# Self and cross attention as one loop over 32 head pairs, with the work between the two loops placed beside pairs of another batch

## Chip, cores and metric

The kernel runs on one core of a Trainium2 chip. The time is device microseconds of that core for one execution; lower is better. Engines: PE (TensorE), DVE (VectorE), ACT (ScalarE), POOL (GpSimd) and SP (SyncE, which issues the DMA here). Each engine works through its own list of instructions in order, and waits for the others at semaphores.

## What is computed

Two blocks on x (2 batches, 512 rows, 128 features) and a context (2 x 154 x 96), all float32. The first block is a small cross attention with 16 heads of 8 with layernorm, GELU feed-forward and residual; the change leaves it as it is. The second block is:

```python
x = _attn(_ln(x, g1, b1), _ln(x, g1, b1), Wq1, Wk1, Wv1, Wo1, bo1) + x   # self: 512 keys
x = _attn(_ln(x, g2, b2), context, Wq2, Wk2, Wv2, Wo2, bo2) + x          # cross: 154 keys
x = _geglu_ff(_ln(x, g3, b3), Wp, bp, Wf, bf) + x                        # a * gelu(gate) @ Wf
```

with 16 heads of 64 in `_attn`, softmax over the keys, and an output projection (1024 to 128). Batches never meet: what batch 1 does in self attention is independent of what batch 0 does in cross attention.

## The kernel before

The 16 heads are taken as 8 pairs, so an attention has 16 pairs (two batches of 8). Each attention is one loop over its pairs. Scores are computed transposed (keys on partitions) in `ph.units` chunks, 4 for self attention (128 keys each) and 2 for cross (77 each). The steps of a pair, with the lines that the profile shows:

- PE `project` (L1011, L1012): queries and keys of a pair, two pairs ahead, into a bank of the ring ST
- ACT `leading` (L487, or L489 and L490 in cross) rounds them into R; DVE `trailing` (L703, or L705 and L706) writes the rest and frees that bank
- PE `scores_max` (L1023) computes the scores of the next pair once for their maxima, DVE `maxima` (L715, L717) reduces them, PE `turn_pair` (L1032) transposes the maxima, ACT `maxima_rows` (L496) copies them
- PE `scores` (L1043) and `less_maxima` (L1052), ACT `exponentials` (L503) into PT, POOL sums them (L384, L388)
- PE `weigh` (L1063) multiplies with the values into PV, half a pair behind; ACT `weighted` (L510) copies PV into AT
- PE `denominators` (L1077) every second pair; after a batch's eight pairs DVE `inverse` (L725) takes the reciprocals, ACT and DVE split them (L515, L729), PE `spread_inverse` (L1086) spreads them over the features, DVE `normalise` (L736) multiplies AT

The ring ST has two PSUM tensors. Every user of it is in one fixed order, and each use waits until the use before the last one is freed. A second ring of two, M, serves the maxima.

For batch 0 the inverse is done inside the loop (pairs 9 to 11), for batch 1 behind it. Between the two loops stand, in this order: inverse and normalisation of batch 1, the values of the context (L1005), the output projection of both batches (`project_out`, L972), and for each batch the residual (L669, L768) and layernorm (`layernorm`, L645 to L659, with ACT's logarithm and exponential L466 and L467 in its middle), the transposes of the result XC (`turn`, L982) and ACT's scaling (L473). Only then does cross attention begin. Behind the cross loop the same steps are followed by GEGLU: `wp` products (L1142, L1143), ACT's Gelu (L558), DVE's product (L783), the last projection (L972) and the output.

Of the kernel before, what the change touches and what calls it, by code (L numbers as in the profile page):

```python
# [22 lines left out]
PAIRS = H // 2  # L23

# [13 lines left out]
def build(nc, a, out):  # L38
    ctx = ExitStack()
    with ctx:  # L40
# [100 lines left out]
        class Phase:  # L141

            def __init__(self, name, rows_of_chunk, chunks):
# [12 lines left out]
                self.den = sem(f"{name}_den")  # L156
                self.rec = sem(f"{name}_rec")
                self.rhi = sem(f"{name}_rhi")
                self.rlo = sem(f"{name}_rlo")
                self.bc = sem(f"{name}_bc")  # L160
                self.norm = sem(f"{name}_norm")

            def spread(self, c):

                return range(4 * c // self.units, 4 * (c + 1) // self.units)

        self_att = Phase("self", P, 4)
        cross_att = Phase("cross", SC, 2)
        self_att.first_turn, cross_att.first_turn = 0, NPAIR


# [4 lines left out]
        o_read = [sem(f"o_read{i}") for i in range(3)]  # L176
# [20 lines left out]
        units, freed = [], {}  # L197

        def unit(key, semaphore, count):
            freed[key] = (semaphore, count)  # L200
            units.append(key)

        for n in range(3):
            unit(("q0", n), full_done, n + 1)
        for n in range(4 * TB):
            unit(("m0", n), m0_free, n + 1)
        for n in range(B * 4):
            for u in range(4):
                unit(("s0", n, u), exp0_done, 4 * n + u + 1)

        def pair_units(ph):
            order = [("proj", 0), ("proj", 1), ("turn", 0)]
            for i in range(NPAIR):
                for c in range(0, ph.units, 2):
                    order += [("st", i, c), ("st", i, c + 1)]
                    if c + 2 == ph.units and i + 2 < NPAIR:
                        order.append(("proj", i + 2))
                    if i == 11:
                        order += [("bc", 0, m) for k in (c, c + 1) for m in ph.spread(k)]
                if i + 1 < NPAIR:  # L220
                    order.append(("turn", i + 1))
            order += [("bc", 1, m) for m in range(4)]
            for key in order:
                if key[0] == "proj":
                    unit((ph.name,) + key, ph.lo, key[1] + 1)
                elif key[0] == "turn":
                    unit((ph.name,) + key, mrow_set, ph.first_turn + key[1] + 1)
                elif key[0] == "bc":
                    unit((ph.name,) + key, ph.norm, 4 * key[1] + key[2] + 1)
                else:  # L230
                    unit((ph.name,) + key, ph.exp, key[1] * ph.units + key[2] + 1)

        unit(("o", 0), o_read[0], B)
        unit(("t", 0), xn_done[0], B)
        for n in range(B * 2):
            unit(("w1", n), gelu_done, 2 * (n + 1))
        unit(("w2",), w2_read, B)
        unit(("t", 1), xn_done[1], B)
        for t in range(NT):
            unit(("v", 0, t), (va_done if t % 2 == 0 else vd_done)[0], t // 2 + 1)  # L240
        pair_units(self_att)
        for t in range(4):
            unit(("v", 1, t), (va_done if t % 2 == 0 else vd_done)[1], t // 2 + 1)
        unit(("o", 1), o_read[1], B)
        unit(("t", 2), xn_done[2], B)
        pair_units(cross_att)
        unit(("o", 2), o_read[2], B)
        unit(("t", 3), xn_done[3], B)
        for n in range(B * 4):
            unit(("wp", n), glu_done, n + 1)  # L250
        unit(("wf",), y_done, B)
        place = {key: n for n, key in enumerate(units)}


        turn0_bank, max_bank = [0], []
        uses = 5
        for n in range(2 * 4 * TB):
            max_bank.append(uses % 2)
            uses += 1
        turn0_bank.append(uses % 2)  # L260
        uses += 1
        for ph in (self_att, cross_att):
            for n in range(2 * ph.units * NPAIR):
                max_bank.append(uses % 2)
                uses += 1

        def bank(key):
            return ST[place[key] % 2]
# [28 lines left out]

        @block.sync
        def _(sp):
# [23 lines left out]

            sp.wait_ge(self_att.proj, NPAIR)
            load("wv2", Wv[0:C, :], a["wv2"])
# [11 lines left out]
        def _(pool):  # L337
# [36 lines left out]
            def sums(ph):  # L374

                for i in range(NPAIR):
                    p = PT1[0:ph.KC, i % 2]
                    s = psums[0:ph.KC, i % 4]
                    pool.wait_ge(ph.exp, ph.units * i + 2)
                    if i >= 4:  # L380
                        pool.wait_ge(ph.den, i // 2 - 1)
                    elif ph is self_att:
                        pool.wait_ge(den0_done, 4 * B)
                    ins = pool.tensor_tensor(s, p[:, 0], p[:, 1], ALU.add)  # L384
                    for c in range(2, ph.NC):
                        link(ins)
                        pool.wait_ge(ph.exp, ph.units * i + c + 1)
                        ins = pool.tensor_tensor(s, s, p[:, c], ALU.add)  # L388
                    ins.then_inc(ph.sum, 1)

            sums(self_att)
            sums(cross_att)

        @block.scalar
        def _(act):
# [66 lines left out]
            def gain_bias(n, g, c):  # L462

                for b in range(B):
                    act.wait_ge(var_done[n], b + 1)
                    link(act.activation(lnv[:, :, :], mv[:, :, 1:2], ACT.Ln))  # L466
                    act.activation(rstd[:, :, :], lnv[:, :, :], ACT.Exp, scale=-0.5).then_inc(rs_done[n], 1)  # L467
                    scale_features(n, g, c, b)

            def scale_features(n, g, c, b):  # L470

                act.wait_ge(t_done[n], b + 1)
                act.activation(xnT[:, b * N:(b + 1) * N], bank(("t", n))[:, b, :], ACT.Identity,  # L473
                               scale=cols[:, g:g + 1], bias=cols[:, c:c + 1]).then_inc(xn_done[n], 1)

            def values(n, tiles, r):
                for t in range(0, tiles, 2):
                    act.wait_ge(v_done[n], t + 1)
                    act.activation(V[0:r, t, :].rearrange("p (u n) -> p u n", u=2), bank(("v", n, t))[0:r],
# [728 lines left out]
```

## Time and profile before

| what | value |
|---|---|
| median of 3 runs | 610.33 us (609.9 to 610.92) |
| the profiled execution, its own time | 609.28 us |
| its span, first to last instruction | 607.4 us |
| PE busy | 534.2 us (88%) |
| DVE, ACT, POOL busy | 276.2, 239.9, 186.2 us |
| mean granted clock of PE | 0.86 of 2.4 GHz |

The span is what the trace covers; all durations below are read against it. Self attention's loop runs from about 175 to 381 us, cross attention's from about 422 to 546 us.

### The profile page before, as it was taken

What the parts mean: (1) busy time and instruction counts of PE and PEld (TensorE: products, weight loads), DVE (VectorE), ACT (ScalarE), POOL (GpSimd) and SP (SyncE); (2) the same over time, 40 slices, a digit from 0 to 9 for tenths busy, and PEclk for the clock granted to TensorE, in tenths of its full rate; (3) what the DMA queues carried; (4) which work ended last, traced back from release to release, by engine and by line L of the source; (5) the groups of instructions that cost most, each with busy time, mean ns of one, the idle gap of its engine ahead of it and who ended that gap; (6) DMA issues with size and microseconds to landing.
All of it is one profiled execution on the core that took longest, in us unless ns stands there. A gap on an engine that the chain in (4) does not pass through costs nothing.

```text
span 607.4 us, 7004 instructions
## 1 busy us (share of the span) xinstructions
PE 534.2 (88%) x2824; PEld 273.4 (45%) x2824; DVE 276.2 (45%) x541; ACT 239.9 (39%) x321; POOL 186.2 (31%) x105
## 2 busy tenths in 40 slices
PE   6889979948778999999999999595799999986797
PEld 3563311226335445455444543274455454435745
DVE  1663430163445555455656550524434355515533
ACT  4433334224223555445544454011355555440131
POOL 4024333200002646656664467000133433330000
PEclk9955555559796999999999999598799999996979
DMA  9300000000000000000000020001000000000001
GB/s 279 127 0 2 0 1 1 1 0 0 0 1 1 2 1 0 1 1 1 0 1 1 2 87 1 0 1 35 0 1 1 2 0 2 1 1 0 1 0 36
DMA packets 7839, 8.95 MB, mean 15 GB/s; under 512 B 544, under 2 KB 6112, under 8 KB 7808
## 3 DMA queue, kind: packets, MB, share of 16 engines
q1 hardware_dynamic: 7808, 8.51, 4.5%
q8 instruction: 23, 0.38, 0.3%
q14 instruction: 8, 0.07, 0.0%
HBM read 7.98 MB, written 0.52 MB: 14 GB/s over the span
## 4 chain that ended last, share of the span: by engine, by line
PE 82%; DVE 13%; ACT 2%; issue 1%; POOL 1%; DMA 1%; SPq 0%; DVEq 0%; POOLq 0%
PE PV L1063 14%; PE ST L1043 11%; PE ST L972 7%; PE ST L1011 6%; PE M L1023 5%; PE PV L933 5%; PE ST L1005 4%; PE ST L1052 4%; PE ST L1032 3%; PE ST L1012 3%; PE DEN L944 3%; PE DEN L1077 3%; PE ST L916 2%; DVE AT L736 2%; PE M L861 2%; PE ST L1142 1%
## 5 line engine op out<-in xcount | busy, mean ns | idle before, releaser
L384 POOL TENSOR_TENSOR psums<-PT 128x1024 f32<-128x1024 f32 (+1 forms) x32 | 75.8, 2370 | 261.5 <-ACT PT L503 261.5
L503 ACT ACTIVATE PT<-ST 128x1024 f32<-128x1024 f32 (+1 forms) x96 | 93.8, 1022 | 44.4 <-PE ST L1052 44.3
L715 DVE TENSOR_REDUCE maxw<-M 128x1 f32<-128x512 f32 x128 | 82.4, 686 | 50.7 <-PE M L1023 50.5
L1063 PE MATMUL PV<-PT,V 128*64 128x512 f32 (+1 forms) x384 | 92.8, 604 | 0.8 <-ACT AT L510 0.8
L1043 PE MATMUL ST<-R 64*128 64x512 f32 (+1 forms) x576 | 86.7, 403 | 1.2 <-DVE R L706 0.6
L388 POOL TENSOR_TENSOR psums<-psums,PT 128x1024 f32<-128x1024 f32 x32 | 75.6, 2362 | 20.8 <-ACT PT L503 19.5
L1043 PEld LDWEIGHTS ST<-R 64*128 64x128 f32 (+1 forms) x576 | 51.4, 176 | 15.8 <-issue 1.6
L1023 PE MATMUL M<-R 64*128 64x512 f32 (+1 forms) x256 | 47.3, 377 | 6.2 <-DVE maxw L715 3.7
L459 ACT ACTIVATE PT<-ST 77x1024 f32<-77x1024 f32 x32 | 31.8, 1018 | 47.8 <-PE ST L916 47.8
L372 POOL TENSOR_TENSOR psums<-PT 77x1024 f32<-77x1024 f32 x12 | 28.1, 2351 | 68.2 <-ACT PT L459 40.8
L1063 PEld LDWEIGHTS PV<-PT,V 128*64 128x64 f32 (+1 forms) x384 | 23.5, 136 | 48.8 <-issue 42.3
L717 DVE TENSOR_REDUCE maxw<-M 128x2 f32<-128x308 f32 x64 | 27.5, 473 | 37.9 <-PE M L1023 37.8
L496 ACT ACTIVATE mrows<-ST 128x512 fp32r<-128x512 f32 x32 | 19.2, 599 | 54.2 <-PE ST L1032 54.2
L1011 PE MATMUL ST<-xnT,Wq 128*128 128x512 f32 x64 | 38.0, 677 | 2.5 <-DVE V L694 1.5
L1052 PE MATMUL ST<-mrows,onesr 64*128 64x512 f32 (+1 forms) x192 | 39.8, 399 | 0.0
L1023 PEld LDWEIGHTS M<-R 64*128 64x128 f32 x256 | 26.0, 192 | 30.4 <-DVE maxw L715 18.1
L933 PE MATMUL PV<-PT,V 77*32 77x512 f32 x128 | 30.7, 1061 | 3.7 <-DVE AT L613 3.7
L510 ACT ACTIVATE AT<-PV 128x512 f32<-128x512 f32 x32 | 19.1, 598 | 36.1 <-PE PV L1063 36.1
L703 DVE TENSOR_TENSOR R<-ST,R 128x1024 fp32r<-128x1024 f32 x16 | 19.6, 1225 | 28.5 <-ACT R L487 28.5
L972 PEld LDWEIGHTS ST<-Wo,AT 128*128 128x128 f32 x256 | 30.8, 202 | 1.6 <-issue 1.3
L972 PE MATMUL ST<-Wo,AT 128*128 128x128 f32 x256 | 30.9, 286 | 0.4 <-DVE AT L736 0.4
L982 PE MATMUL ST<-ident,XC 128*128 128x128 f32 x32 | 7.4, 374 | 23.3 <-DVE XC L659 23.3
(138 smaller groups left out, 625.1 us busy)
## 6 DMA issues: line engine op xcount, KB each, us to landing
Wq<-in_wq SPq DMA_DIRECT2D x2, 512.0 KB, 7.0
Wo<-in_wo SPq DMA_DIRECT2D x2, 512.0 KB, 6.5
xnT<-in_xT SPq DMA_DIRECT2D x2, 256.0 KB, 3.6
psums<-in_sel SPq DMA_DIRECT2D x1, 512.0 KB, 6.9
X<-in_x SPq DMA_DIRECT2D x1, 512.0 KB, 8.2
w<-in_w SPq DMA_DIRECT2D x2, 256.0 KB, 8.3
Wv<-in_wv SPq DMA_DIRECT2D x1, 512.0 KB, 8.9
Wk<-in_wk SPq DMA_DIRECT2D x1, 512.0 KB, 7.7
```

The costliest lines, as they stand in the source:

```text
L384: ins = pool.tensor_tensor(s, p[:, 0], p[:, 1], ALU.add)
L388: ins = pool.tensor_tensor(s, s, p[:, c], ALU.add)
L459: act.activation(PT0[0:SC, n % 2, u % 2, 2 * (u // 2):2 * (u // 2) + 2, :], bank(("s0", n, u))[0:SC, :, :], ACT.Exp, scale=HD0 ** -0.5).th ...
L503: act.activation(PT1[0:ph.KC, i % 2, c], bank((ph.name, "st", i, c))[0:ph.KC, :, :], ACT.Exp, scale=HD ** -0.5).then_inc(ph.exp, 1)
L715: ins = dve.tensor_reduce(maxw[:, i % 2, c, HD * h:HD * h + 1], m[:, :], AX, ALU.max, negate=True)
L933: pe.matmul(PV[32 * g:32 * g + 32, :], V0[:, 2 * b + c, g, 32 * t:32 * t + 32], PT0[0:SC, n % 2, c, g, :], start=(t == 0 and c == 0), stop ...
L972: ins = pe.matmul(u[:, b, t * P:(t + 1) * P], act_tiles[:, m, (TB * b + t) * P:(TB * b + t + 1) * P], w[:, m, :], start=(m == 0), stop=(m ...
L1011: pe.matmul(u[:, 0, :], Wq[:, j * P:(j + 1) * P], xnT[:, b * N:(b + 1) * N], start=True, stop=True)
L1023: ins = pe.matmul(m[:, at:at + ph.NK], r[head(h), 0, qt * P:(qt + 1) * P], r[head(h), 1, 0:ph.NK], start=True, stop=True)
L1043: pe.matmul(u[0:ph.KC, h, :], R[head(h), i % 3, part_k, 1, k], R[head(h), i % 3, part_q, 0, :], start=(part_k + part_q == 0), stop=False)
L1052: ins = pe.matmul(u[0:ph.KC, h, :], onesr[head(h), 0:ph.KC], mrows[head(h), i % 2, :], start=False, stop=True)
L1063: ins = pe.matmul(PV[head(h), :], V[0:ph.KC, b * ph.NC + c, (2 * j + h) * HD:(2 * j + h + 1) * HD], PT1[0:ph.KC, i % 2, c, h, :], start=(c ...
```

## The change

One loop over g = 0 to 31 takes the place of two over i = 0 to 15: pairs 0 to 15 are self attention, 16 to 31 cross attention. The first pairs of cross attention follow the last of self attention without a stop. What stood between the loops is spread over pairs of the other batch. The values of the context are computed in pair 10. The output projection of batch 0 is at the end of pair 12, its residual and layernorm in pair 13; those of batch 1 in pairs 20 and 21. The inverse of self batch 1 is taken in pair 17 and spread in pairs 18 and 19, that of cross batch 0 in pairs 25, 26 and 27. Output projection, residual and layernorm of cross batch 0 are in pairs 28 and 29. Behind the loop stand the GEGLU of batch 0 around the end of batch 1's attention, and then the rest of batch 1. The split of the inverse moves from ACT to DVE (a copy in place of L515), the Gelu writes into PT and not into two buffers, and the load of the context's value weights waits only for the values of self attention.

```diff
@@ PE @@
+            def attention():
...
+                for g in range(NG):
+                    ph, i = pair(g)
                     for c in range(0, ph.units, 2):
-                        if i + 1 < NPAIR:
-                            scores_max(ph, i + 1, c)
-                        if i < NPAIR:
-                            for k in (c, c + 1):
-                                less_maxima(ph, i, k, scores(ph, i, k))
...
+                        for k in maxima_units(g, c):
+                            scores_max(g + 1, k)
+                        scores(g, c)
+                        scores(g, c + 1)
+                        for k in maxima_units(g, c + 1):
+                            scores_max(g + 1, k)
+                        if c + 2 == ph.units and g + 2 < NG:
+                            project(g + 2)
+                        if c >= 2:
+                            weigh(g, c - 2)
+                            weigh(g, c - 1)
...
+                            weigh(g - 1, last - 2)
+                            weigh(g - 1, last - 1)
+                        if g == 10:
+                            loaded("wv2")
+                            values(1, c, SC, ctxT, Wv[0:C, :])
+                            values(1, c + 1, SC, ctxT, Wv[0:C, :])
+                        if g == 11:
+                            spread_inverse(0, c)
+                            spread_inverse(0, c + 1)
+                    if g in (18, 19, 26, 27):
+                        spread_inverse(g // 8 - 1, 2 * (g % 2))
+                        spread_inverse(g // 8 - 1, 2 * (g % 2) + 1)
+                    if g == 12:
+                        attention_out(1, 0)
+                    if g == 13:
+                        turn(("t", 2, 0), 2, 0, None)
+                    if g == 20:
+                        attention_out(1, 1)
+                    if g == 21:
+                        turn(("t", 2, 1), 2, 1, None)
+                    if g == 28:
+                        loaded("wo2")
+                        attention_out(2, 0)
+                    if g == 29:
+                        turn(("t", 3, 0), 3, 0, None)
+                    if g >= 1:
+                        denominators(g - 1)
+                    if g + 1 < NG:
+                        turn_pair(g + 1)
...
+            attention()
+            loaded("wp", "wf")
+            gated(0)
+            weigh(NG - 1, 0)
+            weigh(NG - 1, 1)
+            gated(1)
+            gated(2)
+            denominators(NG - 1)
+            gated(3)
+            for m in range(4):
+                spread_inverse(3, m)
+            pe.wait_ge(glu_done, 4)
+            project_out(("wf", 0), o_read[3], wf_done, AT, wf, 4, 0, 0)
+            attention_out(2, 1)
+            turn(("t", 3, 1), 3, 1, None)
+            for n in range(4, 8):
+                gated(n)
+            pe.wait_ge(glu_done, 8)
+            project_out(("wf", 1), o_read[3], wf_done, AT, wf, 4, 1, 0)
@@ ACT @@
                     for c in range(ph.units):
-                        if i < NPAIR:
-                            exponentials(ph, i, c)
...
-                        if c == 1 and ph.units > 2 and i >= 1:
-                            weighted(ph, i - 1)
-                        if c == ph.units - 1 and i + 2 < NPAIR:
-                            leading(ph, i + 2)
-                        if c == 1 and ph.units == 2 and i >= 1:
-                            weighted(ph, i - 1)
...
+                        exponentials(g, c)
+                        if c == ph.units - 1 and ph.units > 2 and g + 2 < NG:
+                            leading(g + 2)
+                        if c == 1 and g >= 1:
+                            weighted(g - 1)
+                        if c == 1 and g in (13, 21):
+                            root(2, g // 8 - 1)
+                        if c == 1 and g == 29:
+                            root(3, 0)
+                        if c == ph.units - 1 and ph.units == 2 and g + 2 < NG:
+                            leading(g + 2)
+                        if g == 10 and c % 2 == 1:
+                            values(1, c - 1, SC)
@@ DVE @@
+                    for c in range(ph.units):
+                        for k in maxima_units(g, c):
+                            maxima(g + 1, k)
...
+                        if g in (17, 25):
+                            inverse(g // 8 - 1, 2 * c)
+                            inverse(g // 8 - 1, 2 * c + 1)
+                        if c == 0 and g in (10, 18, 26):
+                            inverse_split(g // 8 - 1)
+                        if c == 0 and g == 13:
+                            residual(1, "bo1", 0)
+                        if c == 0 and g == 21:
+                            residual(1, "bo1", 1)
+                        if c == 0 and g == 29:
+                            residual(2, "bo2", 0)
+                        if c == ph.units - 1 and g + 2 < NG:
+                            trailing(g + 2)
...
+                        if c == 1 and g in (18, 19, 26, 27):
+                            normalise(g // 8 - 1, 2 * (g % 2))
+                            normalise(g // 8 - 1, 2 * (g % 2) + 1)
```

(`root` is ACT's part of the layernorm, `gated` the two `wp` products, `attention_out` a `project_out` of one batch, which waits for its four normalisations.)

How this moves instructions, first on ACT in an ordinary cross pair. PT are the exponentials, AT<-PV is `weighted`, the two R rows are `leading` and mrows is `maxima_rows`. Before:

```order
L503 ACTIVATE PT<-ST 77x1024 x2
L489 ACTIVATE R<-ST 128x512
L490 ACTIVATE R<-ST 128x154
L510 ACTIVATE AT<-PV 128x512
L496 ACTIVATE mrows<-ST 128x512
```

Of the change:

```order
L868 ACTIVATE PT<-ST 77x1024 x2
L876 ACTIVATE AT<-PV 128x512
L851 ACTIVATE R<-ST 128x512
L852 ACTIVATE R<-ST 128x154
L858 ACTIVATE mrows<-ST 128x512
```

The copy of PV now stands ahead of the copies into R, in all cross pairs.

Next on DVE the residual and layernorm of cross batch 0 (maxw are the maxima, the R rows `trailing`). Before, behind the loop:

```order
L717 TENSOR_REDUCE maxw<-M 128x2 x4
L725 RECIPROCAL work<-DEN 128x256 x2
L729 SCALAR_TENSOR_TENSOR recw<-recw,cols,work 128x512
L736 TENSOR_TENSOR AT<-ST,AT 128x2x512 x4
L669 TENSOR_TENSOR O<-ST,rows 128x128 x4
L768 TENSOR_TENSOR X<-O,X 128x512
```

Of the change, in pair 29:

```order
L1093 TENSOR_REDUCE maxw<-M 128x2 x2
L1044 TENSOR_TENSOR O<-ST,rows 128x128 x4
L1126 TENSOR_TENSOR X<-O,X 128x512
L1020 BN_STATS st<-X 128x6 x4
L1023 BN_AGGR mv<-st 128x2 x4
L1026 TENSOR_SCALAR mv<-mv 128x4
L1029 TENSOR_TENSOR lnv<-rstd 128x4
L1030 TENSOR_TENSOR lnv<-lnv,mv 128x4
L1031 TENSOR_SCALAR lnv<-lnv 128x4
L1032 TENSOR_TENSOR rstd<-rstd,lnv 128x4
L1034 TENSOR_SCALAR XC<-X,mv,rstd 128x128 x4
L1093 TENSOR_REDUCE maxw<-M 128x2 x2
```

The whole layernorm now stands between the two halves of the maxima of one pair, and pairs 13 and 21 read alike.

Last on ACT the end of the program, behind the last exponentials. Before:

```order
L510 ACTIVATE AT<-PV 128x512 x2
L515 ACTIVATE recw<-work 128x512
L466 ACTIVATE lnv<-mv 128x4
L467 ACTIVATE rstd<-lnv 128x4
L473 ACTIVATE xnT<-ST,cols 128x512
L466 ACTIVATE lnv<-mv 128x4
L467 ACTIVATE rstd<-lnv 128x4
L473 ACTIVATE xnT<-ST,cols 128x512
L558 ACT_TABLE_LOAD
L558 ACTIVATE work<-ST,cols 128x512 x8
```

Of the change:

```order
L910 ACT_TABLE_LOAD
L910 ACTIVATE PT<-ST,cols 128x512
L876 ACTIVATE AT<-PV 128x512
L910 ACTIVATE PT<-ST,cols 128x512 x3
L828 ACT_TABLE_LOAD
L828 ACTIVATE lnv<-mv 128x4
L829 ACT_TABLE_LOAD
L829 ACTIVATE rstd<-lnv 128x4
L834 ACTIVATE xnT<-ST,cols 128x512
L910 ACT_TABLE_LOAD
L910 ACTIVATE PT<-ST,cols 128x512 x4
```

One table load becomes four, two of them around the logarithm of batch 1's layernorm.

## Rows read from the trace of the kernel before

**Rows 1.** Windows: stretch, its length, busy us of PE, PEld, DVE, ACT, POOL, granted clock.

```profile
180.00:200.00 20.00, 16.66 (x65) 9.05 (x66) 11.93 (x18) 5.61 (x6) 6.36 (x3) 0.74 0.00 0
...
220.00:240.00 20.00, 20.00 (x118) 9.48 (x118) 10.19 (x14) 10.08 (x12) 11.78 (x6) 1.00 0.00 1
...
380.00:400.00 20.00, 14.20 (x31) 5.21 (x32) 10.08 (x10) 2.57 (x3) 0.00 (x0) 0.66 0.00 0
```

**Rows 2.** Chain that ended last: start, us, what.

```profile
207.19 1.09 PE ST L1011 x2
...
230.78 1.09 PE ST L1011 x2
...
354.07 1.09 PE ST L1011 x2
...
442.29 1.13 PE ST L1011 x2
...
455.84 1.12 PE ST L1011 x2
...
521.03 1.12 PE ST L1011 x2
...
528.31 1.12 PE ST L1011 x2
```

**Rows 3.** Timeline, PE work that moves: start, us, engine, line, count.

```profile
171.70 1.45 PE L1005 MATMUL ST<-Wv,xnT 128*128 128x512 f32 x3
...
400.60 14.46 PE L972 MATMUL ST<-Wo,AT 128*128 128x128 f32 x128
```

**Rows 4.** Timeline, residual and layernorm of one batch between the loops.

```profile
407.94 0.88 DVE L669 TENSOR_TENSOR O<-ST,rows 128x128 f32<-128x128 f32 x4 [5.93 <-PE ST L972]
...
411.11 0.21 ACT L466 ACTIVATE lnv<-mv 128x4 f32<-128x4 f32 x1 [11.01 <-DVE mv L651]
...
412.39 1.11 DVE L659 TENSOR_SCALAR XC<-X,mv,rstd 128x128 f32<-128x128 f32 x4
```

**Rows 5.** Timeline of one steady cross pair, ACT, DVE and PE.

```profile
504.20 0.60 ACT L489 ACTIVATE R<-ST 128x512 fp32r<-128x512 f32 x1
...
505.02 0.69 DVE L705 TENSOR_TENSOR R<-ST,R 128x512 fp32r<-128x512 f32 x1 [0.22 <-ACT R L490]
...
506.08 0.60 ACT L510 ACTIVATE AT<-PV 128x512 f32<-128x512 f32 x1 [1.09 <-PE PV L1063]
...
506.96 0.66 PE L1032 MATMUL ST<-ident,maxw 128*128 128x128 f32 x4
...
507.83 0.87 PE L1043 MATMUL ST<-R 64*77 64x512 f32 x6
```

**Rows 6.** Timeline of half a self pair.

```profile
318.24 0.66 PE L1032 MATMUL ST<-ident,maxw 128*128 128x128 f32 x4
...
319.36 1.29 DVE L715 TENSOR_REDUCE maxw<-M 128x1 f32<-128x512 f32 x2 [1.59 <-PE M L1023]
...
323.33 0.60 ACT L510 ACTIVATE AT<-PV 128x512 f32<-128x512 f32 x1 [1.08 <-PE PV L1063]
```

**Rows 7.** Timeline, the four normalisations inside the cross loop.

```profile
514.00 4.62 DVE L736 TENSOR_TENSOR AT<-ST,AT 128x1024 f32<-128x1024 f32 x4 [0.79 <-PE ST L1086]
```

**Rows 8.** Timeline of the end.

```profile
550.62 2.08 PE L1086 MATMUL ST<-recw,sel 128*128 128x512 f32 x4 [4.94 <-DVE recw L729]
...
555.96 16.47 PE L972 MATMUL ST<-Wo,AT 128*128 128x128 f32 x128 [0.38 <-DVE AT L736]
...
578.08 1.12 PE L982 MATMUL ST<-ident,XC 128*128 128x128 f32 x4 [5.22 <-DVE XC L659]
...
580.03 1.28 ACT L558 ACT_TABLE_LOAD   x1
...
595.72 7.31 PE L972 MATMUL ST<-wf,AT 128*128 128x128 f32 x64
```

**Rows 9.** Timeline, a short wait of PE.

```profile
181.31 1.39 PE L1023 MATMUL M<-R 64*128 64x512 f32 x2 [2.54 <-DVE maxw L715]
```

More of the change, by code:

```diff
@@ L156, in __init__, with pair, maxima_units @@
                 self.den = sem(f"{name}_den")
[L157 to L169, printed above, removed]
+        self_att = Phase("self", 0, P, 4)
+        cross_att = Phase("cross", NPAIR, SC, 2)
+        def pair(g):
+            ph = self_att if g < NPAIR else cross_att
+            return ph, g - ph.first
+        def maxima_units(g, c):
+            if g + 1 >= NG:
+                return []
+            if pair(g + 1)[0] is pair(g)[0]:
+                return [c]
+            return [c // 2] if c % 2 == 0 else []
+        rec_done = sem("rec_done")
+        recl_done = sem("recl_done")
+        recw_done = sem("recw_done")
+        spread_done = sem("spread_done")
+        norm_done = sem("norm_done")
         o_done = [sem(f"o_done{i}") for i in range(3)]
@@ L175, in build @@
         xn_done = [sem(f"xn_done{i}") for i in range(4)]
-        o_read = [sem(f"o_read{i}") for i in range(3)]
+        o_read = [sem(f"o_read{i}") for i in range(4)]
         w1_done = sem("w1_done")
@@ L194, in build @@
         pool_step = sem("pool_step")
[L197 to L219, printed above, removed]
-                if i + 1 < NPAIR:
[L221 to L231, printed above, removed]
@@ L261, in build @@
[L261 to L265, printed above, removed]
+        ring, max_bank, turn0_bank = {}, [], []
         def bank(key):
-            return ST[place[key] % 2]
+            return ST[ring[key]]
         def head(h):
@@ L464, in gain_bias, with root @@
                 for b in range(B):
[L465 to L470, printed above, removed]
+                    root(n, b)
+                    scale_features(n, g, c, b, bank(("t", n))[:, b, :])
+            def root(n, b):
+                act.wait_ge(var_done[n], b + 1)
+                link(act.activation(lnv[:, :, :], mv[:, :, 1:2], ACT.Ln))
+                act.activation(rstd[:, :, :], lnv[:, :, :], ACT.Exp, scale=-0.5).then_inc(rs_done[n], 1)
@@ L537, in _, with gate @@
+            def gate(n):
+                act.wait_ge(wp_done, n + 1)
+                m = n % 4
+                act.activation(PT[:, 0, n, :], bank(("wp", n))[:, 0, :], ACT.Gelu,
+                               bias=cols[:, COL["bp"] + 4 + m:COL["bp"] + 5 + m]).then_inc(gate_done, 1)
             gain_bias(0, COL["ln_g"], COL["ln_b"])
@@ L546, in _ @@
             gain_bias(1, COL["g1"], COL["c1"])
[L547 to L559 removed]
+            for t in range(0, NT, 2):
+                values(0, t, P)
+            attention()
+            act.wait_ge(cross_att.sum, NPAIR - 1)
+            gate(0)
+            weighted(NG - 1)
+            for n in range(1, 4):
+                gate(n)
+            root(3, 1)
+            scale_features(3, COL["g3"], COL["c3"], 1, bank(("t", 3, 1))[:, 0, :])
+            for n in range(4, 8):
+                gate(n)
         @block.vector
@@ L1148 @@
+            for t in range(1, NT, 2):
+                values(0, t, P)
+            attention()
+            glu(0)
+            glu(1)
+            for part in range(4):
+                inverse(3, part)
+            inverse_split(3)
+            glu(2)
+            glu(3)
+            for m in range(4):
+                normalise(3, m)
+            final(0)
+            residual(2, "bo2", 1)
+            for n in range(4, 8):
+                glu(n)
+            final(1)
 def kernel(**inputs):
```

864 lines of the change are left out of this document (408 added, 456 removed).

## The prediction

> **What bounds the kernel now.** I read the windows first, to see where TensorE (PE) is not busy. Inside either attention loop it is busy for all 20.0 of 20 us at clock 1.00; between the loops it is busy for 14.2 of 20 us, at a mean clock of 0.66 [rows 1]. Then I read the chain that ended last, which gives the rhythm: in each pair of heads one L1011 row, the projection. Two self pairs take 230.78 - 207.19 = 23.6 us (11.8 each), two cross pairs 455.84 - 442.29 = 13.55 us. The cross interval with a denominator step is 528.31 - 521.03 = 7.3 us, the one without it so 6.3 [rows 2]. Last the timelines: who must be ready when PE comes back. PE sets the pace in the loops, so every product added there costs its full time, and every wait added costs too. Outside them the chain runs through DVE and PE in turn.
>
> **What is removed.** From the projection in self pair 13 (354.07) to that in cross pair 1 (442.29) are 88.2 us [rows 2]. In one loop the same stretch is two self intervals (23.6, less about 1.5, my estimate, because cross projections and maxima are narrower), then 6.3 and 7.3: 35.7 us. Removed: 52.5.
>
> **PE work put into the loop.** Values: 16 half-products, three in 1.45 us at most, so 7.0 to 7.7; I take 7.0. Output projections: 128 products in 14.46 for two batches, so 7.2 each, three in the loop: 21.6 [rows 3].
>
> **Residual and layernorm inside a pair (13, 21, 29).** The work of DVE from its first addition to the end of XC is 413.5 - 407.94 = 5.6 us, with ACT's two small instructions in its middle, 3.2 us after the start; from there to the end are 2.4 us [rows 4]. Now three things are in order. (a) The first scores of pair 21 go into the bank that the output projection filled, and DVE reads it only behind maxima (22, 0). A turn starts at 506.96 and scores at 507.83, so 0.9 us later [rows 5]; now reductions and addition end at about 2.9: 2.0 us of wait. (b) ACT does the root behind the copy of PV, and that copy starts when PE's weighing of this pair ends (506.08, released by PV [rows 5]). Weighing ends at about 8.3 on this count (6.3 + 2.0), ACT is done with copy and root at 9.5, XC ends at 11.5. PE has been standing since 8.3, because its next instruction transposes XC. (c) Behind XC on DVE stand maxima (22, 1) and `trailing(23)`, together 1.8 us, which free the bank that the next turn needs: 13.4 against 6.3. So 7.1 us each in pairs 21 and 29. In self pair 13 DVE's two reductions take 1.29 and the copy of PV comes 5.1 us after the turn [rows 6]: 5.1 + 2.5 for (a) + 1.1 to the root's end + 1.9 + 0.65 for the first reduction is 11.3, where the second half of the pair starts at 5.0 now; with a second reduction and the transposes 7.4. Together 21.6. The bounds: 0, if all lay beside PE's work; 3 x 5.6 = 17 if only DVE's time counted; and 22.
>
> **ACT's order in cross pairs.** Before, `leading` (two copies from 504.20, DVE follows at 505.02) stands ahead of the copy of PV (506.08) [rows 5]. Now it stands behind. So it starts when weighing is over: copies end 1.4 us after that, DVE's subtraction 2.4 us after (0.9 of its own), and the next scores need the bank that it frees. They start 0.9 us after weighing without a denominator step and 1.8 with one. Waits of 1.6 and 0.6. Nobody else covers this: PE has only the turn and two maxima to do. It holds plainly in pairs 16, 17 and 22 to 25: 3 x 2.2 = 6.6. The bounds are 0 and 14 pairs x 1.6 = 22.
>
> **The spreading of the inverse.** Two at the end of pairs 18, 19, 26, 27. A normalisation takes 4.62 / 4 = 1.16 to 1.24 us [rows 7]. The second spread needs the bank freed by `trailing` (2.4 us after weighing), the next scores the second normalisation: 2.4 + 1.25 + 1.25 = 4.9 after weighing instead of 1.8 or 0.9, so 3.1 + 4.1 = 7.2 for each batch. Batch 0 of cross attention cost 4.7 before (521.03 - 455.84 = 65.2 for nine intervals that would be 60.5 [rows 2]). Self batch 1 is new: 7.2 + 2.5 = 9.7.
>
> **The end.** From 528.31 to the end (607.4) are 79.1 us. Now, from the projection in pair 29: 17.4 up to where PE stood idle at 545.7, less 0.8 of waiting, plus four gated products (6.9) is 23.5; idle 4.9 [rows 8] + 0.75 for one GEGLU step - 1.75 for a gated product beside it, 3.9; spreads 5.3 (550.62 to 555.96); 3.6 + 7.2 for batch 0's last and batch 1's output projection, and 2.3 at half clock; idle 5.7; one table load that ACT now has between Ln and Exp of the layernorm, 1.3 ([rows 8] have one); transposes and scaling 2.0; four gated steps 9.3 (595.72 - 578.08 - 1.1 = 16.5 for eight, less four of 1.8); 1.5 for the last gate and product with no other batch beside it; batch 1's last projection 3.6; from its end to the end 4.4 (607.4 - 603.0). Sum 73.6, so -5.5.
>
> The Trainium skill ("ScalarE: Activation LUTs", What ACT_TABLE_LOAD costs) puts a switch at about 2.66 us, since it adds a drain to the load. The row above has 1.28 for the load, and no row shows an activation standing right behind one. By the skill the end would be 1.4 us longer.
>
> **Sum without the clock.** -52.5 + 7.0 + 21.6 + 21.6 + 6.6 + 9.7 - 5.5 = +8.5 on the profiled span of 607.4: 615.9.
>
> **The clock.** After PE stood for 2.54 us at 178.8 to 181.3 [rows 9] the mean clock of that 20 us stretch was 0.74; the 4.9 and 5.2 us of [rows 8] were followed by half clock too. The 128 products that take 14.46 us [rows 3] took 16.47 behind the first, 2.0 lost; the eight gated steps took 16.5 where 1.8 each makes 14.4, so some 2.1 to 2.6. I take 2.35 for a fall. Standing times of 3 us or more, or 2.9 within 4.4, now lie in pairs 13, 19, 21, 27 and 29: five falls. Those of 1.9 to 2.4 us (the (a) waits, pairs 18 and 26) are five more, shorter than any that I have a row for; I count one. 6 x 2.35 = 14.1. Bounds: 0 and 10 x 2.35 = 23.5. Span 630.0. The profiled execution took 609.28 for 607.4; the median of the three runs, 610.33, is 2.9 above the span. So 633.
>
> **Rivals.**
> 1. The waits come as worked out, the clock stays at full speed: 615.9 + 2.9 = 619. For it: PE never stands longer than 4 us at one place in the loop. Against: 2.54 us sufficed once [rows 9]. Chance 0.17.
> 2. It is faster. Mechanism: the root and the rest of the layernorm run beside PE's weighing, so that each residual costs only DVE's own time above its slack, about 3.4 instead of 7, and PE does not stand long enough for the clock to fall: 615.9 - 11 + 2.9 = 608, and 601 if ACT's new order costs nothing either. It decides once the waits (37.9 in the sum) and clock losses together are under 29. For it: the merging itself is worth 52.5 against 28.6 of added products. Against: ACT's place behind PV is fixed in its instruction order. Chance 0.09.
> 3. The clock falls in ordinary cross pairs as well, where PE now stands 0.9 and 0.6 us around the maxima, and at all the short waits: three odd pairs and four more, 7 x 2.35 = 16 over the forecast at most, some 645. For it: half clock lasted long in both stretches with frequent waits [rows 1]. Against: waits that short have no fall behind them in the rows. Chance 0.14.
>
> Of rival 3 the Trainium skill ("TensorE: Matmul & The Clock Gate", A second HAM failure mode) tells that frequent short idle times between groups can make the clock swing. No row here shows that for waits as short as 0.9 us.
>
> **Numbers.** Forecast 0.60 (waits and some six falls), rivals 0.17, 0.09, 0.14. The range from 616 to 645 leaves out rival 2 and part of rival 3; the forecast's own is 624 to 640. A change of 0.2% (1.2 us) is about what can be told. Faster 0.08, same 0.03, slower 0.89.
>
> **What would show it.** Right: in the timeline PE idles before the XC transposes of pairs 13, 21, 29 with XC as releaser, for 3 us or more; PE waits for R of `leading`/`trailing` in every cross pair, with two cross intervals at 15.75 instead of 13.55; half clock after the residual pairs; the last 73 us as listed, plus 5.1 of residual 29. Wrong: cross intervals still at 13.55 would take 6.6 and most of the spreads' 9.7 away; a root ahead of the PV copy in time would take 11; a clock of 1.00 throughout pairs 13 to 30 takes 12.

## The result and the profile after

The kernel with one loop takes 640.3 us (median of 4 runs, 639.81 to 642.31), the kernel before 610.12 in the same session (609.21 to 610.92): ratio 1.0507, 95% interval 1.0486 to 1.0527, so 5.1% slower. The forecast was 633 with a range of 616 to 645: the direction and the waits held, and 7 us were missing, which puts the time at the upper edge of the forecast's own 624 to 640, where its third rival begins. The page of the changed kernel, span first, then PE's busy share and the granted clock in 40 slices of 16 us:

```profile
span 637.4 us, 7020 instructions
...
PE   6889979775979999999999879988878988878956
...
PEclk9855555577969999999999979997979978979679
```

From slice 24 on (366.5 us, the first residual) the clock dips again and again, in the middle of what should be dense products. The chain that ended last, with the projection that each pair makes (the answers to [rows 2]; 347.39 is that of pair 12, 377.44 that of pair 13, 555.67 that of pair 29):

```profile
347.39 1.09 PE ST L481 x2
...
377.44 1.20 PE ST L481 x2
...
407.39 1.12 PE ST L481 x2
415.33 1.12 PE ST L481 x2
423.27 1.12 PE ST L481 x2
428.94 1.19 PE ST L556 x2
436.72 1.06 PE ST L481 x2
447.64 1.12 PE ST L481 x2
465.26 1.66 PE ST L481 x2
479.19 1.52 PE ST L481 x2
...
514.37 1.06 PE ST L481 x2
...
539.09 1.06 PE ST L481 x2
555.67 1.13 PE ST L481 x2
```

Two cross intervals (407.39 to 423.27) are 15.88 us, forecast 15.75, before 13.55. PE's waits between 340 and 570 us, by tile, line and releaser (total, times, longest):

```profile
PE ST L556 <- DVE R L1082: 7.0, 4, 1.8
PE ST L432 <- DVE XC L1034: 5.9, 2, 3.0
PE ST L515 <- DVE O L1044: 5.9, 3, 2.3
PE M L494 <- DVE maxw L1091: 3.6, 1, 3.6
PE ST L515 <- DVE R L1082: 3.1, 6, 0.6
PE M L494 <- ACT R L852: 2.4, 3, 0.8
```

These are the waits of the forecast: the spreads of the inverse (L556), the transposes of XC (L432; in pair 13 the wait of 3.6 us for maxw stands in their place), the first scores behind the output projection's bank (L515 <- O), and the ordinary cross pairs (L515 and L494 <- R). None is longer than 3.6 us. The timeline of pair 21, PE, DVE and ACT rows of it (answers to [rows 4, 5]):

```profile
462.04 0.92 PE L515 MATMUL ST<-R 64*77 64x512 f32 x6 [1.83 <-DVE O L1044]
...
467.11 1.94 PE L532 MATMUL PV<-PT,V 77*64 77x512 f32 x8
472.02 0.66 PE L432 MATMUL ST<-ident,XC 128*128 128x128 f32 x4 [2.97 <-DVE XC L1034]
473.71 1.09 PE L503 MATMUL ST<-ident,maxw 128*128 128x128 f32 x4 [1.03 <-DVE R L1082]
```

PE stands for 1.83 us, works 7.0 us, stands for 2.97 and, behind the transposes, for 1.03. How the clock answered is in the windows over the spells that I found below full clock (window, its length, PE busy, ..., granted clock as the third number from the right, after POOL; the sum is that of all eleven windows):

```profile
364.00:367.50 3.50, 3.50 (x15) 1.86 (x14) 0.86 (x7) 2.05 (x2) 0.73 (x1) 0.51 0.00 0
371.00:377.50 6.50, 5.29 (x21) 3.58 (x21) 3.46 (x8) 1.47 (x2) 0.99 (x1) 0.50 0.00 0
429.00:435.50 6.50, 6.50 (x28) 3.09 (x30) 3.02 (x4) 0.66 (x2) 0.00 (x0) 0.50 0.01 3
...
463.00:466.50 3.50, 3.50 (x16) 2.47 (x13) 1.07 (x8) 2.04 (x2) 0.45 (x1) 0.51 0.00 0
473.50:480.00 6.50, 6.29 (x29) 4.14 (x30) 1.71 (x5) 2.64 (x3) 0.01 (x1) 0.50 0.00 1
...
sum 53.50, PE 51.31 PEld 32.19 DVE 20.86 ACT 17.77 POOL 2.19; mean PE 4.66 PEld 2.93 DVE 1.90 ACT 1.62 POOL 0.20
```

There are eleven such spells between 340 and 570 us (the others begin at 442.5, 494, 511, 521, 534.5 and 562), each at 0.50 to 0.53 of full speed, which is the lower level, 1.2 GHz. PE was busy in them for 51.3 us. If all of that takes half as long at full clock, 25.7 us were lost, 2.33 a fall. This estimate is an upper one: e4 below gives 2.1. The forecast took 2.35 a fall and six falls.

PE has ten single waits of 1.75 us and more there, and nine of the spells follow nine of them. The tenth, 1.83 us ahead of the first scores of pair 29 (553.41), has full clock behind it up to 562. The spells at 494 and 511 lie in ordinary cross pairs. By stretch, from the chain's rows, with the time lost as half of PE's busy time in the spells of that stretch:

| from projection of pair | forecast without clock | measured | lost to half clock |
|---|---|---|---|
| 12 to 13 (output projection, residual) | 26.4 | 30.05 | 4.4 |
| 16 to 18 (ordinary cross pairs) | 15.75 | 15.88 | 0 |
| 18 to 20 (four spreads) | 20.8 | 24.37 | 4.9 |
| 20 to 22 (output projection, residual) | 27.9 | 31.55 | 4.5 |
| 22 to 26 (ordinary cross pairs) | 31.5 | 35.18 | 3.4 |
| 26 to 28 (four spreads) | 20.8 | 24.72 | 5.3 |
| 28 to 29 | 16.5 | 16.58 | 0 |
| 29 to the end | 78.7 | 81.7 | 3.2 |

Measured minus forecast is 21.7 in these rows together, against 25.7 lost to the clock: the waits themselves came out some 4 us smaller than forecast, or 1 us if a fall costs 2.1.

### The profile page after: what moved, and what is told of

Read it like the earlier page. It is cut to its first block, busy times and chain, and to the rows that moved or that the text cites. A ratio compares the mean times of both kernels' runs of the same rounds, so it can differ in the third digit from the quotient of the medians.

```text
span 637.4 us, 7020 instructions
## 1 busy us (share of the span) xinstructions
PE 551.7 (87%) x2824; PEld 284.2 (45%) x2824; DVE 276.5 (43%) x549; ACT 240.1 (38%) x320; POOL 185.9 (29%) x105
## 4 chain that ended last, share of the span: by engine, by line
PE 80%; DVE 13%; ACT 4%; issue 2%; DMA 0%; SPq 0%; DVEq 0%; ACTq 0%
PE PV L532 14%; PE ST L515 13%; PE ST L423 6%; PE ST L481 6%; PE M L494 5%; PE PV L386 5%; PE ST L520 4%; PE ST L469 3%; PE ST L503 3%; PE DEN L397 3%; PE ST L482 3%; PE DEN L547 2%; PE ST L369 2%; PE M L313 1%; DVE XC L1034 1%
## 5 line engine op out<-in xcount | busy, mean ns | idle before, releaser
L515 PE MATMUL ST<-R 64*128 64x512 f32 (+1 forms) x576 | 96.7, 439 | 9.5 <-DVE O L1044 5.9
L515 PEld LDWEIGHTS ST<-R 64*128 64x128 f32 (+1 forms) x576 | 56.9, 191 | 26.0 <-issue 10.9
L494 PE MATMUL M<-R 64*128 64x512 f32 (+1 forms) x256 | 51.0, 404 | 9.7 <-DVE maxw L1091 7.3
L494 PEld LDWEIGHTS M<-R 64*128 64x128 f32 x256 | 29.5, 215 | 36.0 <-DVE maxw L1091 20.9
L520 PE MATMUL ST<-mrows,onesr 64*128 64x512 f32 (+1 forms) x192 | 44.0, 432 | 0.0
L1081 DVE TENSOR_TENSOR R<-ST,R 128x512 fp32r<-128x512 f32 x16 | 11.0, 690 | 46.3 <-ACT R L852 46.3
L423 PEld LDWEIGHTS ST<-Wo,AT 128*128 128x128 f32 x256 | 28.9, 192 | 2.4 <-issue 2.4
L432 PE MATMUL ST<-ident,XC 128*128 128x128 f32 x32 | 7.5, 376 | 25.6 <-DVE XC L1034 25.6
```

The source lines that it names most:

```text
L423: ins = pe.matmul(u[:, v, t * P:(t + 1) * P], act_tiles[:, m, (TB * b + t) * P:(TB * b + t + 1) * P], w[:, m, :], start=(m == 0), stop=(m ...
L494: ins = pe.matmul(m[:, at:at + ph.NK], r[head(h), 0, qt * P:(qt + 1) * P], r[head(h), 1, 0:ph.NK], start=True, stop=True)
L515: pe.matmul(u[0:ph.KC, h, :], R[head(h), g % 3, part_k, 1, k], R[head(h), g % 3, part_q, 0, :], start=(part_k + part_q == 0), stop=False)
L520: ins = pe.matmul(u[0:ph.KC, h, :], onesr[head(h), 0:ph.KC], mrows[head(h), g % 2, :], start=False, stop=True)
```

## The experiments

Theory: three orders of instructions make PE wait (ACT's copies into R behind the copy of PV; the residual between the maxima; the spreads), and each wait of about 2 us costs as much again through the clock. Rivals: the waits alone matter and the clock is low for a reason of its own; or what was merged (more products beside one another, more transfers) is slow in itself. The kernel before ran beside each, at 608.85 to 610.12.

| kernel | us, median (all) | ratio to before, 95% |
|---|---|---|
| changed kernel | 640.3 (639.81 to 642.31) | 1.0507 (1.0486, 1.0527) |
| e1_copy_order | 616.12 (615.38 to 616.82) | 1.0103 (1.0078, 1.0129) |
| e2_before_swapped | 631.02 (630.15 to 632.46) | 1.0350 (1.0321, 1.0380) |
| e3_residual_early | 619.93 (619.71 to 620.48) | 1.0167 (1.0144, 1.0191) |
| e4_filled_waits | 631.8 (629.69 to 632.21) | 1.0363 (1.0334, 1.0392) |
| e5_both | 594.66 (594.05 to 594.96) | 0.9758 (0.9736, 0.9780) |
| e6_table | 639.47 (638.57 to 639.93) | 1.0490 (1.0468, 1.0511) |
| e7_best | 582.0 (581.05 to 582.41) | 0.9546 (0.9527, 0.9566) |
| e8_pool_waits | 579.17 (577.78 to 580.54) | 0.9504 (0.9482, 0.9527) |

**e1_copy_order.** The changed kernel with ACT's two orders exchanged in cross pairs:

```diff
-                        if c == ph.units - 1 and ph.units > 2 and g + 2 < NG:
+                        if c == ph.units - 1 and g + 2 < NG:
                             leading(g + 2)
                         if c == 1 and g >= 1:
                             weighted(g - 1)
-                        if c == ph.units - 1 and ph.units == 2 and g + 2 < NG:
-                            leading(g + 2)
```

> The changed kernel (640.3 us) with one edit: ACT's copies of the next pair into R stand ahead of the copy of PV again in cross pairs. If that order costs what the prediction worked out, 6.6 us go in pairs 16, 17 and 22 to 25 and 6.4 in the two pairs of spreading pairs, and cross intervals are 13.55 for two again. If the short waits it makes also let the clock fall (six of the eleven half-clock spells inside the loop lie in pairs 18 to 28 with no residual near), another 8 to 11 us go: 615 to 620. The rival, that the clock falls come only with the residual's waits, gives 627. That PE would have waited for something else anyway gives 635 or more.

One exchange of two ACT instructions gave 24.2 us back. The chain has the old rhythm again:

```profile
409.93 1.12 PE ST L481 x2
417.20 1.12 PE ST L481 x2
423.48 1.12 PE ST L481 x2
```

423.48 - 409.93 = 13.55, as before. The waits of L556, L515 and L494 for R are gone, and between 340 and 570 us five spells at half clock are left, all at pairs 13, 21 and 29. By the chain, the ordinary cross pairs became 10.5 us shorter and the two stretches of spreads 14.2 (24.37 and 24.72 to 17.42 and 17.43). Of these 24.7 us at most 13.2 are the clock (half of PE's 26.4 busy us in the six spells that went), and 11.5 or more are waits. The spreads are not free with this order: each such stretch is still 3.9 us above 13.55, and only their falls and some 4 us of their waits hung on the order.

**e2_before_swapped.** The kernel before with the opposite exchange, in cross attention alone:

```diff
-                        if c == ph.units - 1 and i + 2 < NPAIR:
-                            leading(ph, i + 2)
                         if c == 1 and ph.units == 2 and i >= 1:
                             weighted(ph, i - 1)
+                        if c == ph.units - 1 and i + 2 < NPAIR:
+                            leading(ph, i + 2)
```

> The kernel before (610.1 us) with only that order changed in cross attention: the copy of PV ahead of the copies into R. By my theory 14 pairs wait 1.6 and 0.6 us in turn, 15.4 in sum, and the spreading pair 1.8 more: 627 without any fall of the clock, up to 634 with two or three falls. If the old loop has slack that hides it: 610 to 613.

Slower by 3.5%, with nothing merged: this order alone costs 21.7 us (631.02 against 609.28), some seven tenths of what the change lost. Half clock appeared in it at 466.5, 484, 501, 518 and 535, where the kernel before ran at full clock. The timeline shows what stands ahead of the second of them; the first, third and fourth look the same:

```profile
482.38 0.45 PE L1023 MATMUL M<-R 64*128 64x154 f32 x4 [0.79 <-ACT R L490]
483.43 1.26 PE L1043 MATMUL ST<-R 64*77 64x512 f32 x6 [0.59 <-DVE R L706]
```

And the window behind it:

```profile
484.00:487.00 3.00, 3.00 (x18) 2.19 (x14) 0.05 (x1) 1.17 (x2) 0.00 (x0) 0.50 0.00 0
```

PE stands for 0.79 us, works 0.45 us on the products for the maxima, stands for 0.59 us, and is at half clock 0.4 us after it goes on. But the same two waits at 449.16 and 450.20, and at 555.97 and 557.01, have full clock behind them. In the changed kernel the spells at 494 and 511 have the two waits ahead of them (492.17 and 493.21, 509.51 and 510.55); the same pair of waits at 419.96 and 421.00 had none before 429. The spell at 535 stands behind a single wait of 1.76 us.

**e3_residual_early.** The changed kernel with the additions and moments of the residual at the end of pairs 12, 20 and 28 on DVE, ACT's root ahead of the next pair's exponentials, and only the centring left in pairs 13, 21 and 29:

```diff
+                    if g in (12, 20):
+                        residual_moments(1, "bo1", g // 8 - 1)
+                    if g == 28:
+                        residual_moments(2, "bo2", 0)
...
-                        if c == 0 and g == 13:
-                            residual(1, "bo1", 0)
+                        if c == 0 and g in (13, 21):
+                            centre(2, X, g // 8 - 1)
...
+                    if g in (13, 21):
+                        root(2, g // 8 - 1)
```

> The changed kernel with the residual split: the additions and the moments of the layernorm stand on DVE at the end of the pair in which PE computes the output projection (12, 20, 28), ACT's root stands ahead of the next pair's exponentials, and only the rest (2 us) is left inside pairs 13, 21 and 29. By my theory the three pairs lose some 15 of their 21.6 us of waits, and five or six clock falls with them go, 11 to 13 us: 612 to 616. If only the waits count and the clock falls for other reasons: 625. If the waits move to another place: 635 or more.

20.4 us gained, 4 less than the lower end of what I expected. The waits for O are gone, but one spell at half clock stayed in pair 13 (367.5 to 371), behind a wait of 2.1 us for maxw that I had not foreseen; e8 takes it up. Seven spells are left in the loop, four fewer than in the changed kernel. One of them (415.5) lies in an ordinary cross pair where the changed kernel had none. In pairs 21 and 29 PE now waits for R ahead of the turn:

```profile
464.90 0.63 PE L503 MATMUL ST<-ident,maxw 128*128 128x128 f32 x4 [1.83 <-DVE R L1091]
```

Neither this wait nor its like at 546.84 has half clock behind it, though waits of 1.76 us have, at the spreads of the same run.

**e4_filled_waits.** The changed kernel with products that nobody reads in pairs 21 and 29: two of 128x512 into PV ahead of the first scores, three into the transposes' bank ahead of the wait for XC.

```diff
+                        if g in (21, 29):
+                            pe.wait_ge(cross_att.pvs, g - 17)
+                            for k in range(2):
+                                pe.matmul(PV[:, :], ident[:, :], ...)
                         scores(g, c)
...
-                        turn(("t", 2, 1), 2, 1, None)
+                        turn(("t", 2, 1), 2, 1, None, 3)
...
-                        turn(("t", 3, 0), 3, 0, None)
+                        turn(("t", 3, 0), 3, 0, None, 3)
```

(The last argument is the number of products that `turn` puts ahead of its wait.)

> The changed kernel with extra products that nobody reads in pairs 21 and 29: two of 128x512 into PV where PE waits for the output projection's bank, three into the transposes' bank where it waits for XC. The waits stay as long as they are. If PE's standing makes the clock fall, the four half-clock spells of these pairs (19.7 us of busy time at half clock) go and the time drops by 8 to 10: 630 to 632. If the clock doesn't depend on it: 640 to 641.

More work on PE, 8.5 us less time. Windows over the two places in pair 21 (compare 463.00 and 473.50 above), over the output projection of pair 28, and over the transposes of pair 29:

```profile
463.00:466.50 3.50, 3.50 (x22) 1.86 (x20) 1.04 (x8) 1.95 (x2) 1.27 (x1) 1.00 0.00 0
471.00:480.00 9.00, 7.88 (x54) 3.96 (x52) 2.85 (x8) 4.61 (x7) 2.35 (x1) 1.00 0.00 1
532.00:538.00 6.00, 6.00 (x43) 4.25 (x42) 1.10 (x3) 1.31 (x4) 2.35 (x1) 1.00 0.00 0
558.00:568.00 10.00, 10.00 (x60) 3.79 (x55) 0.87 (x2) 5.50 (x7) 4.70 (x2) 1.00 0.00 0
```

All at 1.00, and what PE waits for comes no earlier: the first scores of pair 21 start at 462.01 (462.04 in the changed kernel), and the transposes 2.97 us behind the end of the weighing, as before. So it is PE's standing that lets the clock fall, at a wait as short as 1.83 us. The expectation counted four spells in these pairs; the changed kernel has three (463, 473.5 and 562), for the fourth (534.5) lies in pair 27 behind the second spread, and e4 still has it. By the chain, the stretch from pair 20 to 22 became 3.8 us shorter (31.55 to 27.75) and that from pair 29 to the end 2.4 (81.7 to 79.3): 6.2 us for three falls, 2.1 each.

The profiled execution is 10.2 us shorter than that of the changed kernel, and 3.4 of these lie in pairs 22 to 26, where nothing was edited. The two spells of the changed kernel at 494 and 511 are missing here, with the same waits in place:

```profile
487.91 0.45 PE L499 MATMUL M<-R 64*128 64x154 f32 x4 [0.79 <-ACT R L861]
488.95 0.92 PE L520 MATMUL ST<-R 64*77 64x512 f32 x6 [0.59 <-DVE R L1091]
```

So part of the gain is not that of the filled places, and what those short waits bring hangs on something that these runs don't show.

**e5_both.** e1 and e3 together.

> Both edits in the changed kernel: ACT's copies into R first, the residual's moments early. If they are separate costs that share the clock, the waits left in the loop are 1 us each in pairs 13, 21, 29 and 4 per spreading, and PE never stands long enough for half clock before the end: 637.4 - 13 - 17.6 - 25 + some 3 is a span of 585, so 585 to 591. If the one hid part of the other (each alone took 24 and 20 us), simple addition gives 596; if some wait that neither removes keeps the clock falling: 600 or more.

The two gains add up (24.2 + 20.4 = 44.6; measured 45.6), and the merged loop is now 2.4% faster than the kernel before, so what was merged is not slow in itself. The time is nearest to the 596 of simple addition and 4 us above the 585 to 591 that I expected. In the loop one wait of 2.11 us and the spell behind it (369.5 to 373) are left, both in pair 13. The waits of 0.94 us at 431.24 and 498.13, behind the spreads, have no fall.

**e6_table.** The changed kernel with ACT told to load the table set of the exponential and the logarithm ahead of the last layernorm, so that no load stands between Ln and Exp:

```diff
             for n in range(1, 4):
                 gate(n)
+            act.preload_act_table_set(exp_ln)
             root(3, 1)
```

> The changed kernel with one table set that has both Ln and Exp loaded behind batch 0's Gelu, so that no load stands between the logarithm and the exponential at the end. By the trace the load took 1.28 us there with the exponential right behind it: 639.0, at most 2.5 less than the changed kernel where the clock's phase helps. If a switch costs 2.66 us, 637.7. If PE's way is not through it: 640.3.

The timeline of ACT at this place, first of the changed kernel, then of e6:

```profile
611.62 0.21 ACT L828 ACTIVATE lnv<-mv 128x4 f32<-128x4 f32 x1 [22.86 <-DVE mv L1026]
611.84 1.28 ACT L829 ACT_TABLE_LOAD   x1
613.14 0.20 ACT L829 ACTIVATE rstd<-lnv 128x4 f32<-128x4 f32 x1
```

```profile
613.28 0.21 ACT L828 ACTIVATE lnv<-mv 128x4 f32<-128x4 f32 x1 [22.86 <-DVE mv L1027]
613.52 0.20 ACT L829 ACTIVATE rstd<-lnv 128x4 f32<-128x4 f32 x1
```

Exp starts 0.02 us behind the end of the load: the load costs its 1.28 us and nothing more. The medians differ by 0.8 us, less than these runs can tell apart; PE's wait for XC is 6.92 us in the one and 5.65 in the other, 1.27 shorter. The Trainium skill ("ScalarE: Activation LUTs", What ACT_TABLE_LOAD costs) puts the switch at about 2.66 us with a drain. The trace does not show that drain here: the load starts as Ln ends (611.83), and Exp follows its end.

**e7_best.** e5 with the table of e6, and the end in another order: denominators ahead of the gated products 1 to 3, the inverse ahead of the second GEGLU step, the output projection and residual of cross batch 1 ahead of the last projection of batch 0.

```diff
-            gated(1)
-            gated(2)
             denominators(NG - 1)
+            gated(1)
+            gated(2)
             gated(3)
...
+            attention_out(2, 1)
             project_out(("wf", 0), o_read[3], wf_done, AT, wf, 4, 0, 0)
-            attention_out(2, 1)
...
-            glu(1)
             for part in range(4):
                 inverse(3, part)
+            glu(1)
...
-            final(0)
             residual(2, "bo2", 1)
+            final(0)
```

> Both edits, the single table, and another order of the end: denominators ahead of three gated products, so that the reciprocals start 3 us earlier, and batch 1's output projection ahead of batch 0's last one, so that this one (3.6 us) fills PE's wait for the residual. By my count of the end 1.3 + 2.8 + 2.3 us less than both edits alone, and one clock fall shorter: 578 to 583. If the end is bound by DVE's chain whatever PE does in it: 585 or more.

12.7 us less than e5, 4.5% faster than the kernel before. Of the half clock behind 200 us one spell remained, in pair 13. DVE's and POOL's rows there, then PE's:

```profile
364.30 3.17 DVE L1042 TENSOR_SCALAR XC<-X,mv,rstd 128x128 f32<-128x128 f32 x4
...
364.79 2.34 POOL L744 TENSOR_TENSOR psums<-PT 128x1024 f32<-128x1024 f32 x1 [11.86 <-ACT PT L868]
...
368.13 1.39 PE L494 MATMUL M<-R 64*128 64x512 f32 x2 [2.11 <-DVE maxw L1099]
```

The four TENSOR_SCALAR took 3.17 us instead of 1.12; one of them took 2.397 us where the median is 0.343. It is the third: it starts at 364.82, 0.03 us after POOL's sum, and the fourth starts at 367.13, where that sum ends. The wait of 2.07 us ahead of the last transposes of XC (559.96) has full clock behind it.

**e8_pool_waits.** e7, where GpSimd's first sum of pair 13 starts only once XC is written:

```diff
+                if g == 13:
+                    pool.wait_ge(xc_done[2], 1)
                 ins = pool.tensor_tensor(s, p[:, 0], p[:, 1], ALU.add)
```

> The version with all reorderings, where GpSimd's first sum of pair 13 additionally waits until VectorE has written the normalised rows XC of batch 0. In that version VectorE's four TENSOR_SCALAR X -> XC took 3.17 us there (1.12 in pair 21), one of them 2.397 us where the median is 0.343, while GpSimd's TENSOR_TENSOR of 2.34 us ran from 364.79 to 367.13; TensorE then waited 2.11 us for maxw and went at half clock from 368.0 to 371.5. Theory: the one VectorE instruction stood still for as long as GpSimd's ran. Then XC falls back to 1.1 us, TensorE's wait before the maxima of pair 14 all but goes (0 to 0.3 us), the clock does not fall, and the span is 2.1 + 1.7 = 3.8 us shorter: 574.8 (median 578.2). Sum psums of pair 13 ends some 1.5 us later, which the denominators, a pair later, do not need. Rival: the long TENSOR_SCALAR has another cause (ScalarE's reads, or the record); then XC stays near 3.2 us, and the span at 578.6.

```profile
367.07 1.12 DVE L1044 TENSOR_SCALAR XC<-X,mv,rstd 128x128 f32<-128x128 f32 x4
...
368.36 2.37 POOL L746 TENSOR_TENSOR psums<-PT 128x1024 f32<-128x1024 f32 x1 [12.67 <-DVE XC L1044]
```

XC takes 1.12 us, PE's wait for maxw is gone, and so is the spell: none is left behind 200 us while PE works. From the first output projection in the chain (351.89 in e7, 354.66 here) to the end are 226.7 and 223.4 us, 3.3 less, where I expected 3.8. The whole span fell by only 0.5 (578.6 to 578.1), because in this execution the stretch ahead of that, which the edit does not touch, came out 2.8 us longer. The medians differ by 2.8, of which 1.2 may be the session: the kernel before differs by as much (610.09 and 608.85).

## Why the forecast was right, and what it mis-sized

- **What is removed, and the products put in.** As forecast: the stretch from pair 28 to 29, an interval, an output projection and one (a) wait, is 16.58 for 16.5.
- **ACT's order in cross pairs.** Right in mechanism and size: 15.88 for 15.75, and e1 gives 13.55 back. But the term had only the waits of the six ordinary pairs, 6.6 us; e1 gained 24.2 and e2 lost 21.7. The rest is the falls of the clock, 13 us at most, and some 4 us of the spreads' waits.
- **The spreads.** Their term, 7.2 a batch, was too large: with the clock taken out the two stretches are 5.9 above 13.55 each. Against the 4.7 that one batch cost before, that is 7.1 us for the 9.7 of the sum.
- **Residual and layernorm in pairs 13, 21, 29.** Right: PE stands at O (1.8 to 2.3 us) and at XC (3.0) or maxw (3.6), as worked out from ACT's root behind the copy of PV. The three terms of 7.1 to 7.4 were high by 0.6 to 1 each: the waits and the transposes come to 6.1 to 6.5. That ACT's place is what decides, e3 shows (20.4 us).
- **The clock: the term that was mis-sized.** The forecast expected five falls behind standing times of 3 us or about it, and all five came, those of pairs 19 and 27 behind single waits of 1.75 us. Of the five places with 1.9 to 2.4 us "I count one"; four brought a fall (the (a) waits of pairs 13 and 21, pairs 18 and 26), and the (a) wait of pair 29 none. Two more came in ordinary cross pairs behind waits of 0.79 and 0.59 us. So eleven falls for six, 22.8 us (at 2.1) to 25.7 us for 14.1. That is 9 to 12 us more, less 1 to 4 for waits that came shorter: the 7 us by which the time was above the forecast. The nearness of the total is in part luck, for the two errors have opposite signs. e4 shows that the standing is the cause and not something that goes with it.
- **A row that was overlooked.** The prediction says of the short waits that it has no row for any. The trace of the kernel before has one, at the start of cross attention, with the window behind it:

```profile
429.48 0.83 PE L1023 MATMUL M<-R 64*128 64x154 f32 x4 [1.83 <-DVE maxw L717]
...
431.00:437.00 6.00, 6.00 (x29) 4.04 (x30) 1.43 (x4) 2.52 (x3) 0.00 (x0) 0.50 0.00 0
```

The clock was full at 429.5 to 430 and at half from 430.5 on, with one more wait of 0.57 us in between. Read with this row, the five short waits would have counted for more than one fall.

- **The end.** 78.7 forecast, 81.7 measured; the fall at 562 to 569 (3.2 at most) is about the difference. The table load cost 1.3, as the row had it.
- **Rivals.** That the clock stays up was wrong: it fell more often, not less. The third rival, falls at all the short waits and in ordinary cross pairs too, came true for the most part: four of its five short places and two of its three odd pairs. Seven falls over the forecast would by its own price be 649 and not the 645 that it names; five came, and shorter waits paid for a part of them. The faster case named as its mechanism a root that runs in time; it does not in this order, and with e3 it does: with both orders mended the merged loop is about 15 us faster than the kernel before, 28 with the end reordered too, and 30 with pair 13 mended as well.

What stays open: when a short wait brings a fall. The pair of waits of 0.79 and 0.59 us stands in 18 places of five traces (the changed kernel, e2, e3, e4, e6), and half clock came behind 10 of them. The same place in the same loop has it in one kernel and not in the other.

## What to carry to other kernels

An in-order engine that serves two consumers decides by its order which of them waits: put the copy whose input is there first, and the one that must wait for the bottleneck engine's current product behind it. When work of one stage is moved beside another, look at what stands between its steps on each serving engine, since TensorE pays for most gaps of about 2 us twice, once standing and once at half clock. So count the gaps first and then price them, the clock with them. Here two orders of instructions made a merging that is worth 2.4% (with the end reordered as well, 4.5 to 5%) into a loss of 5%.

## What the runs showed of the hardware

- TensorE's granted clock fell to its lower level (1.2 GHz) behind single waits well under 3 us. In the ten traces, from 350 us on, half clock came behind 29 of 36 single waits of 1.75 to 2.3 us, and behind all ten waits of 2.97 to 3.58 us inside the loop. It came behind 10 of 18 pairs of waits of 0.79 and 0.59 us, and behind none of 12 waits of 1.46 to 1.56 us. A fall lasted 3 to 7 us and cost 2.1 us (three filled in e4) to 2.33 us at most (half of PE's busy time, mean of eleven). The Trainium skill ("TensorE: Matmul & The Clock Gate", A second HAM failure mode) tells of a clock that swings with frequent short idle times. The eleven spells look like that, and e4 ended three of them by filling the gaps with unread products.
- A VectorE TENSOR_SCALAR of 0.343 us stood still while a GpSimd TENSOR_TENSOR of 2.34 us ran, and took 2.397. The Trainium skill ("SBUF — State Buffer", Who interferes with whom) says that the two engines share a pair of ports which one instruction holds to its end, and counts tensor_scalar among VectorE's operations that can need it; e8 agrees (1.12 us without the overlap, 3.17 with it).
- ACT_TABLE_LOAD between two activations took 1.28 us with 0.02 us behind it.
